# Expert stage: routing weights, input and output turned in squares by VectorE and carried through DRAM

## The reference

```python
logits = x2 @ gate_w.T                      # 16 experts
scores = sigmoid(logits); sc = scores + bias_e
# groups of 4 experts: sum of each group's best two; the best 2 of 4 groups are kept
# of their experts the best 4 by sc; weight = score / (sum of the four) * 2.5
def body(acc, inp):
    wu, wd, cw = inp                        # one expert: up, down, its column of weights
    y = relu2(x2 @ wu.T) @ wd.T             # 64 hidden features, relu squared
    return acc + cw[:, None] * y, None
routed = scan(body, zeros_like(x2), (up_w, down_w, combine.T))
shared = relu2(x2 @ shared_up.T) @ shared_down.T     # 256 hidden features
out = routed + shared
```

## Time and profile before

| what | value |
| --- | --- |
| median of 3 runs | 2152.15 us (2149.84 to 2154.32) |
| the profiled execution | 2151.95 us, its span 2150.1 us |
| PE busy | 2047.2 us, 95% |
| DVE busy | 1650.3 us, 77% |
| ACT busy | 1438.3 us, 67% |
| POOL busy | 618.3 us, 29% |
| DMA | 35.30 MB in 32834 packets |

### The profile page before, as it was taken

How to read it: one execution, slowest core, us unless ns; L and a number is a source line. 1 busy time by engine, 2 the same in 40 slices (tenths; PEclk the granted TensorE clock), 3 DMA queues, 4 the chain that set the end, 5 groups by cost and what they waited for, 6 DMA issues and landing times. The chain is left out here.

```text
span 2150.1 us, 40463 instructions
## 1 busy us (share of the span) xinstructions
PE 2047.2 (95%) x14885; PEld 1372.3 (64%) x14885; DVE 1650.3 (77%) x4015; ACT 1438.3 (67%) x1931; POOL 618.3 (29%) x862
## 2 busy tenths in 40 slices
PE   3899999999999999997999999799999996999998
PEld 1577777777777777775444444577777773444443
DVE  3888888888888888874566665577777776999997
ACT  1687877778887777873666666466666663555554
POOL 1345444544544454552000000133333331000000
PEclk9999999999999999997999999899999997999999
DMA  5000000000000000001000000000000000000000
GB/s 165 21 21 21 21 11 21 21 21 21 21 21 11 21 21 21 21 21 55 1 0 1 1 1 1 1 2 2 2 2 2 2 2 1 10 16 11 15 11 20
DMA packets 32834, 35.30 MB, mean 16 GB/s; under 512 B 6864, under 2 KB 26496, under 8 KB 32640
## 3 DMA queue, kind: packets, MB, share of 16 engines
q1 hardware_dynamic: 32640, 32.73, 5.8%
HBM read 11.75 MB, written 4.19 MB: 7 GB/s over the span
## 5 line engine op out<-in xcount | busy, mean ns | idle before, releaser
L864 POOL TENSOR_SCALAR_AFFINE_SELECT pr<-pr 128x512 f32<-128x512 f32 x256 | 202.2, 813 | 370.7 <-ACT pr L795 370.7
L422 PE MATMUL a_pO<-va,pr 128*128 128x66 f32 x2048 | 304.6, 272 | 1.9 <-POOL pr L864 1.5
L422 PEld LDWEIGHTS a_pO<-va,pr 128*128 128x128 f32 x2048 | 273.7, 193 | 18.9 <-issue 15.4
L1628 ACT ACTIVATE c_pr<-c_pS 128x1536 f32<-128x1536 f32 x128 | 186.0, 1453 | 119.3 <-PE c_pS L1440 119.3
L1683 POOL TENSOR_SCALAR_AFFINE_SELECT c_pr<-c_pr 128x512 f32<-128x512 f32 x256 | 158.0, 641 | 265.4 <-DVE c_pr L1548 265.4
L761 ACT ACTIVATE sq<-a_pW 128x512 f32<-128x512 f32 x192 | 114.4, 597 | 145.4 <-PE a_pW L363 142.7
L789 ACT ACTIVATE th<-a_pS 128x1536 f32<-128x1536 f32 x128 | 185.9, 1453 | 30.1 <-PE a_pS L407 29.6
L423 PE MATMUL a_pO<-va,pr 128*128 128x66 f32 x1024 | 199.0, 276 | 0.0
L795 ACT ACTIVATE pr<-th 128x1536 f32<-128x1536 f32 x128 | 190.5, 1488 | 3.1
L407 PE MATMUL a_pS<-qs,k 128*128 128x512 f16 (+1 forms) x1024 | 187.3, 326 | 0.9 <-issue 0.9
L1548 DVE TENSOR_SCALAR c_pr<-c_pr 128x1536 f32<-128x1536 f32 x128 | 122.6, 958 | 78.4 <-ACT c_pr L1628 78.4
(11 more groups left out here) (259 smaller groups left out, 4509.1 us busy)
## 6 DMA issues: line engine op xcount, KB each, us to landing
k<-k SPq DMA_DIRECT2D x64, 256.0 KB, 3.6
x<-in_L_attn_tokens_dram SPq DMA_DIRECT2D x8, 512.0 KB, 6.8
out_dram<-x SPq DMA_DIRECT2D x16, 256.0 KB, 2.3
d_h<-in_L_ffn_h_w_dram SPq DMA_DIRECT2D x2, 1024.0 KB, 7.4
wmod<-in_L_wmod_dram SPq DMA_DIRECT2D x2, 384.0 KB, 4.0
d_w<-in_L_ffn_w_w_dram SPq DMA_DIRECT2D x3, 256.0 KB, 3.2
a_wq<-in_L_attn_Wq_dram SPq DMA_DIRECT2D x1, 512.0 KB, 7.1
a_wkv<-in_L_attn_Wkv_dram SPq DMA_DIRECT2D x1, 512.0 KB, 6.9
```

What stands on the lines that cost most here:

```text
L422: pe.matmul(out, w[:, hh * N + t * P:hh * N + (t + 1) * P], v[:, 0, p, :], start=True, stop=t == 0)
L864: last = gp.affine_select(out=part, in_=part, compare_op=ALU.is_ge, fill=0.0, base=0, pattern=[[0, HPG], [1, P]], channel_multiplier=-1)
L1628: act.activation(pr[g][:, :, :], pS[:, :, 0:N + P], ACT.Exp, scale=float(1.0 / np.sqrt(np.float32(DQ)))).then_inc(s_ex, 1)
```

## The change

TensorE keeps only the up, down and logit products. The rest of the turning and spreading goes another way:

- **Weights.** VectorE turns the 16 columns of weights, now fp32, in squares of 32x32 (L1204 of the changed code, STREAM_TRANSPOSE). SP writes them to a DRAM tensor by_expert in four transfers and reads them back in four, each of 4 rows of 2 KB to 64 partitions, every row read once per partition, so that the weights of a unit lie spread over its 128 hidden features in SBUF (cwB, 8 units x 512 tokens, two buffers). Units 2 to 5 wait for the first two reads (cw0), units 6 to 9 for the last two (cw1).
- **Input.** VectorE turns the normalised x in squares (L1133), SP writes it to x_turned in four transfers and reads it back in one; ScalarE shifts and scales it from SBUF.
- **Output.** The same with og: turned by VectorE (L1218), out_turned, back to SBUF as `out`, from which VectorE adds (L1223).
- **Buffers and order.** pU has four banks instead of two, hT three buffers, s two. The input of a run is normalised three iterations ahead and shifted, routed and chosen two ahead; the weights are made one iteration ahead. The addition of run n-1 stands between products 6 and 7 of run n. At the start of the stage SP first carries x of runs 0 and 1, then issues the MLP's loads.

```diff
+        def sp_put_in(sp, n):
+            sp.wait_ge(s_xt, n + 1)
+            if n >= 1:
+                sp.wait_ge(s_xh, 16 * n)
+            for j in range(S4):
+                sp.dma_start(x_turned[:, :, j, :].rearrange('g s c -> s g c'), xt[SQ * j:SQ * (j + 1), :, :, :].rearrange('s g t r -> s g (t r)')).then_inc(s_xd, 16)
+
+        def sp_get_in(sp, n):
+            sp.wait_ge(s_xd, 16 * S4 * (n + 1))
+            if n >= 1:
+                sp.wait_ge(s_hT, n)
+            sp.dma_start(xh[:, :, :, :].rearrange('p j t r -> p (j t r)'), x_turned.rearrange('g s j c -> (g s) (j c)')).then_inc(s_xh, 16)
...
+        def sp_get_out(sp, n):
+            sp.wait_ge(s_od, 16 * S4 * (n + 1))
+            if n >= 1:
+                sp.wait_ge(s_st, ADD_STEPS * (n - 1) + 1)
+            sp.dma_start(out[:, :, :, :].rearrange('p g t s -> p (g t s)'), out_turned.rearrange('j r g c -> (j r) (g c)')).then_inc(s_out, 16)
+
+        def sp_put_weights(sp, n):
+            sp.wait_ge(s_cT, n + 1)
+            if n >= 1:
+                for part in s_cw:
+                    sp.wait_ge(part, 2 * 16 * n)
+            for j in range(S4):
+                sp.dma_start(by_expert[:, :, j, :], cwT[SQ * j:SQ * j + E, :, :]).then_inc(s_cd, 16)
+
+        def sp_get_weights(sp, n):
+            sp.wait_ge(s_cd, 16 * S4 * (n + 1))
+            if n >= 2:
+                sp.wait_ge(s_a, RT * (n - 1))
+            rows = by_expert.rearrange('(k j y) t g r -> k y j (t g r)', k=2, y=2)
+            for k in range(2):
+                for y in range(2):
+                    sp.dma_start(cwB[n % 2][EI * y:EI * (y + 1), RT // 2 * k:RT // 2 * (k + 1), :],
+                                 rows[k, y].unsqueeze(0).broadcast_to((EI, RT // 2, W))).then_inc(s_cw[k], 16)
+
         @block.sync
         def _(sp):
+            for n in range(2):
+                sp_put_in(sp, n)
+                sp_get_in(sp, n)
             ahead(sp)
+            for n in range(-1, RUNS + 1):
+                if 0 <= n + 1 < RUNS:
+                    sp_put_weights(sp, n + 1)
+                if 2 <= n + 2 < RUNS:
+                    sp_get_in(sp, n + 2)
+                if 0 <= n + 1 < RUNS:
+                    sp_get_weights(sp, n + 1)
+                if 0 <= n - 1 < RUNS:
+                    sp_put_out(sp, n - 1)
+                    sp_get_out(sp, n - 1)
+                if 2 <= n + 3 < RUNS:
+                    sp_put_in(sp, n + 3)
...
-            pe.matmul(pC[j % 2][:, :], sel[:, j, :], cwT[n % 2][:, :], start=True, stop=True).then_inc(s_cb, 1)
+            pe.matmul(pU[(IT * n + u) % 4][:, :], uT[:, t * P:(t + 1) * P], hT[n % 3][:, :], start=True, stop=True).then_inc(s_up, 1)
...
-            dve.tensor_tensor(a[(IT * n + u) % 4][:, :], q[j % 4][:, :], pC[j % 2][:, :], ALU.mult).then_inc(s_a, 1)
+            dve.tensor_tensor(a[(IT * n + u) % 4][:, :], q[j % 4][:, :], cwB[n % 2][:, j, :], ALU.mult).then_inc(s_a, 1)
+
+        def dve_turn_out(dve, n):
+            dve.wait_ge(s_og, n + 1)
+            if n >= 1:
+                dve.wait_ge(s_od, 16 * S4 * n)
+            dve.transpose(ot[:, :, :, :].rearrange('p j t s -> p (j t s)'), og[:, :, :, :].rearrange('p j t r -> p (j t r)')).then_inc(s_ot, 1)
 
         def dve_add(dve, n):
-            dve.wait_ge(s_oT, n + 1)
-            add_to_x(dve, c, s_st, n, T4, pB[:, :])
+            dve.wait_ge(s_out, 16 * (n + 1))
```

More of the change, by code:

```diff
@@ L943, in moe @@
         S2 = 2
+        SQ = 32
         RUNS = B // S2
@@ L948, in moe @@
         ROW = E + EG
-        RSTEPS = 32
+        RSTEPS = 30
         HIGH, TAKEN = 3.0e38, -3.0e38
@@ L989, in weights_of @@
         def weights_of(u):
             return RT + u if u < ST else u - ST
-        def pe_front(pe, n):
-            pe.wait_ge(s_xn, n + 1)
-            if n >= 1:
-                pe.wait_ge(s_hT, n)
-            for t in range(T4):
-                last = pe.transpose(pX[:, t * P:(t + 1) * P], xn[:, t, :], c.id32[:, :])
-            last.then_inc(s_xT, 1)
         def pe_route(pe, n):
@@ L1002, in pe_route @@
             if n >= 1:
-                pe.wait_ge(s_cw, n)
+                pe.wait_ge(s_ex, n)
             for t in range(T4):
-                last = pe.matmul(pR[:, t * E:(t + 1) * E], hT[n % 2][:, t * P:(t + 1) * P], gT[:, :], start=True, stop=True)
+                last = pe.matmul(pR[:, t * E:(t + 1) * E], hT[n % 3][:, t * P:(t + 1) * P], gT[:, :], start=True, stop=True)
             last.then_inc(s_lg, 1)
-        def pe_turn_weights(pe, n):
-            pe.wait_ge(s_rt, RSTEPS * (n + 1))
-            out = pR[:, BANK // 2:BANK].bitcast(F16)
-            for t in range(T4):
-                last = pe.transpose(out[:, t * P:(t + 1) * P], cwp[:, t, :], c.id16[:, :])
-            last.then_inc(s_cT, 1)
         def pe_up(pe, n, u):
@@ L1039, in pe_down @@
             pe.matmul(pD[:, :], dT[:, t * D:(t + 1) * D], a[(IT * n + u) % 4][:, :], start=u == 0, stop=u == IT - 1).then_inc(s_dn, 1)
-        def pe_back(pe, n):
-            pe.wait_ge(s_og, n + 1)
-            if n >= 1:
-                pe.wait_ge(s_st, 4 * n - 3)
-            for t in range(T4):
-                last = pe.transpose(pB[:, t * P:(t + 1) * P], og[:, t * P:(t + 1) * P], c.id32[:, :])
-            last.then_inc(s_oT, 1)
         @block.tensor
@@ L1061, in _ @@
             pe.wait_ge(s_taken, len(turns))
-            pe.wait_ge(s_k, 4)
-            for n in range(-1, RUNS + 1):
+            for n in range(-2, RUNS + 1):
                 if 0 <= n < RUNS:
@@ L1203, in _ @@
             dve.wait_ge(s_km, 4)
-            for n in range(-1, RUNS + 1):
+            dve_normalise(dve, 0)
+            dve_normalise(dve, 1)
+            for n in range(-2, RUNS + 1):
                 if 0 <= n - 1 < RUNS:
                     dve_weigh(dve, n - 1, 9)
-                if 0 <= n < RUNS:
-                    dve_weights(dve, n)
                 if 0 <= n + 1 < RUNS:
-                    dve_normalise(dve, n + 1)
+                    dve_weights(dve, n + 1)
                 if 0 <= n < RUNS:
```

166 lines of the change are left out of this document (78 added, 88 removed).

## The result

The changed kernel takes **2299.65 us**, the median of four runs (2297.77 to 2304.24), against 2153.18 of before, timed beside it: a ratio of 1.068, 95% interval [1.067, 1.070]. The forecast was 2282, with a range of 2205 to 2335. The profiled execution has a span of 2298.2 us, 148.1 more than before, where the sum of the forecast had +130.

A forecast was written before the change was run, and what follows sets the result against it. TensorE bounds the old loop; afterwards a closed path through VectorE and SP, 18.95 + 9.45 = 28.4 us, sets the period. Fourteen periods +104, start +24, end +2 on 2152 give 2282 us, range 2205 to 2335.

The forecast's parts named there:

- What bounds the kernel before; 2.8 us less per run for TensorE: Expert loop: TensorE, busy 20.90 of 20.90 us, sets the pace; without spread products and turns it needs 18.1 of 20.94.
- The circle through VectorE, SP and VectorE: Expert loop, once per run: weights' turn, SP's transfers, output read back, addition, next weights; 28.4 us, lower bound of the period.
- VectorE's part, 9.45: From the addition through products, choice and normalising to the end of the next weights' turn on VectorE: 9.45 us.
- The transfers' part, 18.95: From the weights' turn through weights' writes, spread reads, output's writes and read back to the addition: 18.95 us.
- They come behind the spread reads in the same queue: The output's four writes wait on SP's queue for 2.10 MB of spread reads, landing at 15.95 us, over 6 after issue.
- Another wait lies inside the circle without lengthening it: ScalarE's shift of x waits ahead of square 3: product 3 at 7 us, output's turn at 7.9 instead of 6.
- rival 1: Spread reads go at 361 GB/s or don't hold up the output's writes: period 23.95 us, 2220 in all; chance 0.22.
- VectorE's longest wait is the addition's, 6 to 8 us: Sign to look for: VectorE's addition waits for the output's read, 6 to 8 us each, about 14 times.
- The start, +24: Start of the expert stage: product 9 of run 0 at about 1062 instead of 1038.2, +24 us.
- The sum: Whole kernel: fourteen longer periods +104, start +24, last run and end +2, together +130 us on 2152.
- The faster one: Transfers hide and TensorE sets the pace at 18.1 us a run: about 2141 us; chance 0.05.
- Rival 3: Spread reads below 218 GB/s, or the granted clock falls: slower still, 2416 us at half the rate; chance 0.08.

The follow-up runs named there:

- the last experiment: by_expert and x_turned doubled in DRAM, against the changed kernel reordered (addition of run n-2, x written and read earlier, MLP loads last): 2143.2 us, ratio 0.995.
- run 0: Not a follow-up kernel: the first of the expert loop's sixteen runs of two samples; its product 9 is at 1066.23 in the changed kernel, 1038.06 before.

## Why the prediction was right, point by point

- **What bounds the kernel before; 2.8 us less per run for TensorE.** Right, by the last experiment: 18.51 in place of 20.94, 2.4 us.
- **The circle through VectorE, SP and VectorE sets the period.** Shown by three cuts, each of which keeps the spread reads as they are: the addition a run later (-86 us), the output first (-60), the output by TensorE (-73). It is 29.7 us long, 28.4 in the forecast. The other signs: the spread reads run near 218 GB/s; TensorE is busy 77% of the stretch, two thirds in the forecast, since a part of its work runs at the lower clock.
- **VectorE's part, 9.45.** Measured 9.23. The turns cost 0.63 (1212.99 to 1213.62), forecast 0.60, and 0.31 for the small one, forecast 0.23.
- **The transfers' part, 18.95.** Measured 20.55, the term that was mis-sized. Nearly all of it is in the stretch from the first spread read's issue to the landing of the output's writes, 14.2 us where 12.35 were counted; the read back gives 0.4 of it back. The forecast gave the queue 2.36 MB there, and it had 2.62: the read of x, in the forecast a wait beside the circle, has its 0.26 MB ahead of the spread reads. At the forecast's 218 GB/s they are 1.2 of the 1.9 us, an estimate; the rest is the rate, which was 187 GB/s in the first 2 us, 204 to 215 then, and had a tail. Fourteen times 1.3 us are 18, as much as from 2282 to 2300, because the start and the end, both off, nearly cancel (below).
- **"They come behind the spread reads in the same queue".** The result, writes that land over 6 us after their issue (7.6), is right, and the reason isn't shown: from GpSimd's own queue they are nearly as late (6.9), and its packets don't start while the reads fill the engines. The price was the same here, which is luck as far as the reason goes: it would have led to a cure that gives nothing.
- **"Another wait lies inside the circle without lengthening it".** Right for the changed kernel: product 3 comes 7.2 us after the weights' turn (forecast 7), the output is turned at 8.5 (7.9). But it is a circle of its own, 23.4 us long, and hardly shorter than the 23.95 given for rival 1. The forecast counted no price for TensorE's stop in it: 3.0 us of waiting and 1.6 of lower clock. It put most of TensorE's idle time ahead of down 7; that wait is 2.94 us (before 1237.58), no longer than this one. So the prediction's sign "VectorE's longest wait is the addition's, 6 to 8 us" came out only in part: 3.0 to 5.7 in the middle, 10.7 once, and product 3's are as long (5.2 to 6.2).
- **The start, +24.** Measured +28.2 (product 9 of run 0 at 1066.23 against 1038.06). ScalarE had shifted run 2's x by 1051.02 (forecast 1050). From there the forecast counted seven units, 12.0 us, to product 9; it took 15.2. From product 3 (1051.57) to product 8 (1062.94) it was 11.4 us where five units are 8.6, and from there to product 9 3.3 where one is 1.7, since VectorE's list has the normalising between. TensorE had stood for 20 us before, and its gate products show the lower clock (granted 0.50 from 1051 to 1056):

```profile
1051.07 1.89 PE L1061 MATMUL b_pR<-b_gT,b_hT 128*128 128x16 f32 x8 [20.40 <-ACT b_hT L1283]
```

- **The sum.** The start is 4 us and fourteen periods 18 us over the forecast; what is left, in the first and last runs and the end, gives some 5 back. Together 148 for 130. That the first and the last of these nearly cancel is luck.
- **The rivals.** The faster one (transfers hide, TensorE sets the pace) was priced at 2141. It exists, but not in this order of work: with both circles and the DRAM buffer apart it is 2143. Rival 1's case, reads at the rate of 128 partitions, is the one with own rows over 128 partitions: 2240 measured, of which some 10 were expected for its copy at the start, for 2220. Rival 3's fall of the clock came too (0.87 on the mean over the steady part), but the two measured parts of the circle, 9.23 and 20.55 us, hold no term of it.

## What to carry to other kernels

When work is moved from a full engine to a path through DRAM, don't add up busy times; draw each closed path through the lists of the engines and the issuing queue, with every wait for a buffer to be free, those in DRAM included. Here four such numbers (29.7, 23.4, 19.5, 18.5 us) came one after the other, each hidden by the last, and only when the order and the DRAM buffers had cut three of them did the 2.4 us saved on TensorE show in full. Then count what the path costs where nothing lies beside it: 23 us at the start against 31 gained by the whole loop.

## What the runs showed of the hardware

- A second queue gave no way past full DMA engines: four 64 KB writes issued while 2.1 MB of reads were under way landed 6.9 us later from GpSimd's queue (median), 7.6 from SP's, and 1.8 when they were issued ahead of the reads. None of the packets of GpSimd's queue started in the 4.9 us shown in which SP's reads kept the engines full.
- DRAM to SBUF ran at 209 to 242 GB/s into 64 partitions and at 393 to 426 into 128 with rows of each partition's own, in packets of 8 KB; with rows shared by all partitions, in packets of 2 KB, at 204 to 215 and 272 to 328.
- After TensorE had stood still for 3.0 us, the gate products and one large product ran at full speed, and the next two at about half, 1.60 and 1.71 us for 0.86, with a granted clock of 0.57 to 0.58 in 1224 to 1228. The wait's second price was over half of its first.
- VectorE's turn in squares cost 0.63 us from start to start for 128x512 in fp32 (0.71 long), as much as a multiplication, and 0.31 for 128x128.
